# Moving a normalization from VectorE to ScalarE in the preparation of a four-layer graph network

## The reference

```
h = maximum(layernorm(x), 0)                    # (6250, 128)
edge_feat = concat(h[src], h[dst])              # (106250, 256)
g = gelu(edge_feat @ mlp_w1 + mlp_b1)           # 64 hidden
w = sigmoid(g @ mlp_w2 + mlp_b2)                # one weight per edge
...                                             # degrees from w, then
out = segment_sum((h @ conv_w)[src] * norm, dst) + conv_b
x = x + out                                     # three more layers of this kind
```

## Time and profile before

| | |
|---|---|
| median of 3 runs | 4262.63 us (4259.69 to 4265.24) |
| the profiled execution, own time | 4269.07 us |
| its span, first to last instruction | 4267.3 us |
| mean granted clock of TensorE | 0.804 |
| busy share: PE, DVE, ACT, POOL | 75%, 52%, 46%, 52% |
| preparation, to the end of line 1442 | 119.3 us |

### The profile page before, as it was taken

One profiled execution on the slowest core, in us unless ns is written; L12 is line 12 of the kernel. 1 busy time (PEld: TensorE's weight loads), 2 busy tenths in 40 slices (PEclk: granted clock), 3 DMA queues, 4 the chain that ended last, 5 costly groups with the idle time before them and its releaser, 6 DMA issues.

```text
span 4267.3 us, 68479 instructions
## 1 busy us (share of the span) xinstructions
PE 3218.4 (75%) x19874; PEld 2621.2 (61%) x19874; DVE 2219.3 (52%) x9829; ACT 1973.3 (46%) x2929; POOL 2238.3 (52%) x1830
## 2 busy tenths in 40 slices
PE   4666667644454466676899419998999999999999
PEld 3455555433333355565687317887777788888888
DVE  6766666544444599998211001266444444444444
ACT  2222222211111255555899419964444455555555
POOL 3777777777777888888888888811000000000000
PEclk6555555555555599998999759999999999999999
DMA  4899997444444599995999549964776788888897
GB/s 132 287 310 310 302 314 220 109 109 106 100 107 108 131 233 235 232 235 118 222 240 264 112 64 255 260 193 151 218 221 205 218 264 255 252 263 253 273 295 245
DMA packets 874024, 898.42 MB, mean 211 GB/s; under 512 B 186010, under 2 KB 807169, under 8 KB 873664
## 3 DMA queue, kind: packets, MB, share of 16 engines
q1 hardware_dynamic: 700656, 785.25, 59.4%
q0 software_dynamic: 168464, 107.01, 15.4%
q10 hardware_dynamic: 4544, 1.77, 0.2%
HBM read 699.91 MB, written 193.86 MB: 209 GB/s over the span
## 4 chain that ended last, share of the span: by engine, by line
PE 40%; POOL 30%; issue 13%; DVE 12%; DMA 4%; ACT 1%; SPq 0%; DVEq 0%; POOLq 0%; ACTq 0%
PE ps L1191 27%; POOL adj L792 22%; POOL rows L784 8%; PE ps L1096 5%; PE ps L1078 3%; DMA adj<-scattering 3%; DVE same L1456 2%; DVE pre L1492 1%; DMA pieces<-adj 1%; DVE scaled L1496 1%; DVE wide L1808 1%; PE ps L1259 1%; PE ps L1264 1%; ACT wide L977 1%; PE ps L1187 1%
## 5 line engine op out<-in xcount | busy, mean ns | idle before, releaser
L1191 PE MATMUL ps<-wide,tab 128*128 128x512 f32 (+2 forms) x7644 | 1730.1, 383 | 50.7 <-DVE wide L1808 42.1
L1191 PEld LDWEIGHTS ps<-wide,tab 128*128 128x128 f32 x7644 | 1373.7, 189 | 355.4 <-DVE wide L1808 63.0
L977 ACT CAST wide<-pieces 128x1536 fp32r<-128x1536 f16 (+5 forms) x1026 | 1245.8, 1258 | 743.6 <-PE ps L1191 553.5
L792 POOL DMA_INDIRECT adj<-scattering x832 | 1310.1, 1575 | 253.7 <-issue 243.7
L784 POOL DMA_INDIRECT rows<-table,src_of x880 | 843.6, 959 | 319.3 <-issue 260.0
L1808 DVE CAST wide<-pieces 128x1024 fp32r<-128x1024 f16 (+3 forms) x604 | 397.0, 663 | 577.0 <-PE ps L1191 573.8
L1096 PE MATMUL ps<-dst_mlp,onehot_t 128*128 x2640 | 364.5, 232 | 142.1 <-DVE pre L1492 92.5
L824 POOL DMA_DIRECT2D out<-scattering x13 | 9.8, 754 | 838.3 <-DVE scattering L1773 838.3
L1096 PEld LDWEIGHTS ps<-dst_mlp,onehot_t 128*128 128x128 bf16 x2640 | 274.9, 104 | 221.8 <-issue 163.5
L1456 DVE SCALAR_TENSOR_TENSOR same<-ps,key,first_weight 128x128 bf16<-128x128 f32 x832 | 284.9, 344 | 228.3 <-PE ps L1078 227.9
L908 ACT ACTIVATE onehot<-plain,norm 128x128 f32<-128x128 bf16 x880 | 280.9, 390 | 227.0 <-DVE norm L1562 227.0
(11 more groups left out here) (262 smaller groups left out, 3542.1 us busy)
## 6 DMA issues: line engine op xcount, KB each, us to landing
pieces<-adj SPq DMA_DIRECT2D x550, 640.0 KB, 5.3
pieces<-adj SPq DMA_DIRECT2D x121, 512.0 KB, 4.8
h_rows<-rows SPq DMA_DIRECT2D x220, 256.0 KB
rows<-h_rows SPq DMA_DIRECT2D x220, 256.0 KB
onehot_list<-onehot_b SPq DMA_DIRECT2D x220, 128.0 KB, 2.8
low_row<-low_list SPq DMA_DIRECT2D x220, 128.0 KB
plain<-onehot_list SPq DMA_DIRECT2D x220, 128.0 KB
pieces<-adj SPq DMA_DIRECT2D x54, 480.0 KB, 4.6
```

The source lines that it names most:

```text
L792: nc.gpsimd.indirect_dma_start(out=adj[:, :], out_offset=bass.IndirectOffsetOnAxis(ap=place[:, k:k + 1], axis=0), in_=count16[:, k:k + 1], ...
L977: nc.scalar.copy(to, of).then_inc(cast_act, 1)
L1191: last = nc.tensor.matmul(ps_sum[SUMMED[u] % 2][:, 0:b * P], tab[q % 2][:, c, half, :], of, start=(c == u0 and half == 0), stop=(kind == " ...
```

## The change

- ScalarE writes h itself, one instruction per block, from x: Relu(x * rstd - mean * rstd), scale and bias per partition. For the bias, invert_roots computes node_shift = -mean * rstd on VectorE. norm_nodes leaves VectorE and relu_nodes ScalarE; the semaphore node_fed goes, node_scaled comes.
- TensorE transposes h, so that the copy out of PSUM needs no Relu; this copy and all that follows it lags one chunk more.
- The first half's roots are inverted as soon as they are there; ScalarE takes the second half's roots in front of its fourth chunk (ROOTS_AT = 3).
- SyncE stores the edge lists between the two halves of x instead of behind x.
- The edge rows are read at chunk 6 instead of 8.
- The 23 later weights are issued behind the chunks on ScalarE's queue; TensorE waits for them in front of the first layer's end, ScalarE behind its last weighing.

```diff
+        node_shift = room[:, 0:NW]
...
-        STEPS_READ = 8
+        STEPS_READ = 6
+        ROOTS_AT = 3
...
             for k, (b0, b1) in enumerate(X_PIECES):
+                if k == len(X_PIECES) // 2:
+                    sp.wait_ge(rows_in, 16 * 6)
+                    for e in range(2):
+                        sp.dma_start(edge_list[e].rearrange("(c p) j -> p c j", p=P), rows_i[:, e, :, :]).then_inc(lists_stored, 16)
                 sp.dma_start(x[:, b0:b1, :], a["x"][b0 * P:b1 * P, :].rearrange("(b p) d -> p b d", p=P)).then_inc(x_in[k // 2], 16)
             sp.wait_ge(pads_set, 3)
             sp.dma_start(x[0:N % P, whole, :], a["x"][whole * P:N, :]).then_inc(x_in[-1], 16)
-            sp.wait_ge(rows_in, 16 * 6)
-            for e in range(2):
-                sp.dma_start(edge_list[e].rearrange("(c p) j -> p c j", p=P), rows_i[:, e, :, :]).then_inc(lists_stored, 16)
...
-            for where, what in loads:
-                act.dma_start(where, what).then_inc(weights_in, 16)
-            for n, (b0, b1) in enumerate(STAT):
+            def take_node_roots(n):
+                b0, b1 = STAT[n]
                 act.wait_ge(variances, n + 1)
                 nc.scalar.activation(node_rstd[:, b0:b1], node_rstd[:, b0:b1], ACT.Sqrt).then_inc(roots_set, 1)
-            def relu_nodes(i):
+            def take_later_roots(i):
+                if i == ROOTS_AT:
+                    take_node_roots(1)
+            def norm_nodes(i):
                 b0, b1 = node_blocks(i)
-                act.wait_ge(node_fed, i + 1)
-                nc.scalar.activation(h[:, b0:b1, :], node_pre[:, i % 2, 0:b1 - b0, :], ACT.Relu).then_inc(h_set, 1)
+                act.wait_ge(node_scaled, 1 if b1 <= STAT[0][1] else 2)
+                for b in range(b0, b1):
+                    last = nc.scalar.activation(h[:, b, :], x[:, b, :], ACT.Relu, bias=node_shift[:, b:b + 1], scale=node_rstd[:, b:b + 1])
+                last.then_inc(h_set, 1)
...
-                nc.scalar.activation(node_t[:, i % 2, 0:(b1 - b0) * P], ps_node_t[:, i % 2, 0:(b1 - b0) * P], ACT.Relu).then_inc(node_turned_sb, 1)
+                nc.scalar.copy(node_t[:, i % 2, 0:(b1 - b0) * P], ps_node_t[:, i % 2, 0:(b1 - b0) * P]).then_inc(node_turned_sb, 1)
...
-            pipeline(MC, [(2, take_first_part), (0, relu_nodes), (0, copy_nodes)])
+            take_node_roots(0)
+            pipeline(MC, [(0, take_later_roots), (3, take_first_part), (0, norm_nodes), (1, copy_nodes)])
+            for where, what in loads:
+                act.dma_start(where, what).then_inc(weights_in, 16)
...
-            act.wait_ge(weights_in, 16 * LOADS)
             act.wait_ge(steps_set, 1)
...
             for g in range(GROUPS):
                 weigh(g)
+            act.wait_ge(weights_in, 16 * LOADS)
...
             def turn_nodes(i):
                 b0, b1 = node_blocks(i)
-                pe.wait_ge(node_fed, i + 1)
+                pe.wait_ge(h_set, i + 1)
                 after(pe, node_turned_sb, i - 1)
                 for b in range(b1 - b0):
-                    last = nc.tensor.transpose(ps_node_t[:, i % 2, b * P:(b + 1) * P], node_pre[:, i % 2, b, :], ident[:, :])
+                    last = nc.tensor.transpose(ps_node_t[:, i % 2, b * P:(b + 1) * P], h[:, b0 + b, :], ident[:, :])
...
-            pipeline(MC, [(0, turn_nodes), (1, multiply_nodes), (1, turn_steps)])
+            pipeline(MC, [(0, turn_nodes), (1, multiply_nodes), (2, turn_steps)])
...
-            pe.wait_ge(weights_in, 16 * LOADS)
             pe.wait_ge(zero_set, 2)
             add_no_degrees(True)
...
             pe.wait_ge(added, GROUPS * S)
+            pe.wait_ge(weights_in, 16 * LOADS)
...
                 link(nc.vector.reciprocal(node_rstd[:, b0:b1], node_rstd[:, b0:b1]))
+                nc.vector.scalar_tensor_tensor(node_shift[:, b0:b1], node_moments[:, b0:b1, 0], -1.0, node_rstd[:, b0:b1], ALU.mult, ALU.mult
+                                               ).then_inc(node_scaled, 1)
...
             nc.vector.tensor_copy(tile_of[:, :], ps_tile_t).then_inc(tile_of_set, 1)
+            invert_roots(0)
             dve.wait_ge(x_in[1], 48)
             node_stats_of(1)
-            invert_roots(0)
...
-            def norm_nodes(i):
-                b0, b1 = node_blocks(i)
-                after(dve, node_turned, i - 1)
-                after(dve, h_set, i - 1)
-                for b in range(b0, b1):
-                    last = nc.vector.tensor_scalar(node_pre[:, i % 2, b - b0, :], x[:, b, :], node_moments[:, b, 0:1], node_rstd[:, b:b + 1],
-                                                   ALU.subtract, ALU.mult)
-                last.then_inc(node_fed, 1)
...
-            pipeline(MC, [(2, take_src), (0, norm_nodes), (0, read_steps), (2, split_nodes), (3, take_steps)])
+            pipeline(MC, [(0, take_src), (0, read_steps), (0, split_nodes), (3, take_steps)])
```

More of the change, by code:

```diff
@@ L451, in build @@
         roots_set = sem("roots_set")
-        node_fed = sem("node_fed")
+        node_scaled = sem("node_scaled")
         h_set = sem("h_set")
```

## The result

The changed kernel took 4240.2 us (median of 5 runs, 4237.23 to 4243.74), the kernel before 4260.3 us (5 runs, 4259.38 to 4265.24): ratio 0.9949, 95% interval 0.9935 to 0.9964, that is 20.1 us faster, between 15.3 and 27.7. The forecast was 4238 (4230 to 4250). The profiled execution of the changed kernel took 4243.74 us, that of before 4269.07; these two lie 25.3 us apart.

The account below looks back on a forecast made before the run. The preparation ahead of the edge loop, paced by VectorE/TensorE to 762 us, was taken to set the end. Chunks from 32.0 plus 33.5 end at 65.5 instead of 90.34: 4262.63 - 24.8 = 4237.8 us, forecast 4238 (4230 to 4250).

Parts of the forecast that it names:

- The bound and its release: Preparation ahead of the edge loop: shorter by d, it ends the kernel d earlier if both starts move along.
- Loads: Start of the kernel: first half's statistics begin at 14.5 us (13.3 to 15.8) instead of 18.52, VectorE's first chunk at 32.0.
- the earlier landing of the lists: Loads at the start: without the weights between, the lists could land at 6.5 us instead of 9.05.
- The round: Walk through 13 chunks: a round is the largest engine's share, ScalarE's 2.35 us, not the sum of 4.4.
- the three cold rounds: Start of the chunk walk: TensorE at 1.2 GHz for about three rounds, adding 3 x 0.5 = 1.5 us.
- the slower rival: Chunk walk: stages stay in series, 6.3 us a round, 19 us late, 4282 us; decides from 4.5 us; chance 0.03.
- signs named for being wrong: Rounds over 3 us, ScalarE idle before first parts, another group loop or scatter pace, first edge copy waiting for ScalarE's queue.
- The clock: TensorE in the chunk walk: fewer pauses, so 1.2 GHz for about three rounds more, then rounds of 2.35 us.
- Due dates: Edge rows read at chunk 6 and weights issued behind the chunks cost nothing: 7 and at least 11 us of cover.
- the first term of the sum: End of the old chunk walk, line 1395, at 90.34 us; less the predicted 65.5 it gives 24.8 us.
- GpSimd's lead of 15.8 us: Edge loop to 762 us: GpSimd's 25 waits for line 1492, 15.8 us together, taken as up to that much lead.

Follow-up runs that it names:

- loop_alone: The changed kernel with its loads in their old places and edge rows read at chunk 8: 4242.62 us against 4261.7 for the kernel before, ratio 0.9953.
- move_no_lag: The changed kernel, normalization still on ScalarE, with the old lags: 4262.36 us, ratio 1.0001 to the kernel before.
- lags_alone: The kernel before with the new lags alone, VectorE still normalizing, now ahead of the taking: 4257.89 us, ratio 0.999.
- before_a: The kernel before, unchanged, profiled once more: walk 59.1 us, line 1395 at 86.2 us.
- experiment 3: Two runs of the changed kernel with GpSimd's first table gather made to wait longer: 4245.65 and 4259.47 us beside 4238.55.
- before_b: The kernel before, unchanged, profiled another time: walk 58.8 us, line 1395 at 86.8 us.
- again: The changed kernel, unchanged, run once more: 4238.55 us against 4259.57 for the kernel before, ratio 0.9951.
- gathers_late: The changed kernel with GpSimd's first table gather waiting for changed_set, beginning 14.3 us later: 4245.65 us beside 4238.55.
- gathers_later: The changed kernel with GpSimd's first table gather waiting for the keys, beginning 27.9 us later: 4259.47 us beside 4238.55.
- split_lag: The changed kernel with VectorE's splitting one chunk behind: 4239.74 us.
- lay_later: The changed kernel with splitting one chunk behind, ahead of the edge rows' reading, and the steps' layout behind two takings: 4239.31 us against 4259.39, ratio 0.995.

## Why the prediction was right, and where it was off

**The bound and its release.** That the preparation's end sets the end of all was right: the end of the walk, the keys and the first addition moved by 25.0, 25.0 and 25.1 us between the two profiles, the span by 25.3. The predicted 4244.2 for an execution like the profiled one met 4243.74. That the median of 4240.2 met 4238 as well has some luck in it: the gain was 20.1 us instead of 24.8, and the kernel before took 4260.3 us in five runs instead of the 4262.63 of three that the forecast started from.

**Loads.** The first statistics were predicted for 14.5 us, between 13.3 and 15.8, and came at 15.72: the upper bound. The term that failed is the earlier landing of the lists (8.94 us instead of 6.5 or a middle of it). With the weights out of the way they land as late as before, and from 6 to 8 us the DMA engines were busy only 0.39 of the time before and 0.38 after, which the mean of 0.86 over 18.5 us doesn't show. What the lists wait for stays open. x was early enough, as loop_alone shows from the other side (waits of 2.31 and 1.03 us come back). The first taking came at 32.98 instead of 32.0.

**The round.** Four normalizations took 1.65 us, as worked out; the round 2.27 instead of 2.35. Of the three cold rounds, a number that no row of before gives, one shows in VectorE's walk: it waits 1.00 us for TensorE at 38.33 us, where 1.5 were set aside. The walk from the first taking was 32.4 us instead of 33.5, while that taking came 1.0 late; so line 1395 met its 65.5 (65.34) by two small errors against each other. That the round would be the largest share and not the sum hangs on the lags. move_no_lag shows that the slower rival was a real mechanism: with the old lags a round took 4.09 us at the high clock and 5.36 at the low one, beyond the 4.5 from which it was to decide in part of the rounds only, and this ate the whole gain. There the trace agrees with the rule of the Trainium skill ("ScalarE: Activation LUTs", "Rules for kernel authors": relu, addition and multiplication belong on VectorE): four normalizations took 1.65 us on ScalarE against 1.11 on VectorE, and the move gained nothing. In the changed order the dearer engine was the right one, since 1.65 us ran beside the others' work and 1.11 us of VectorE would have been added to its 2.0 (lags_alone).

One of the signs named for being wrong did show: ScalarE is idle in front of six first parts, longest at 33.43 us (2.92) and 60.33 us (3.00). VectorE comes late there, behind the steps' layout, the last slow products of TensorE, the reading and the taking of the edge rows, or at the walk's end; the rounds between, such as the one from 41.08 us, have no such wait, so the stages don't stand in series.

**The clock.** The reason given for its level, the pauses, doesn't hold. before_a ran from 48.35 to 67 us at 1.00 with a pause of 1.61 us or more in every round (TensorE busy 9.30 of 18.65 us); the profile of before shows the same pauses at 0.50 from 43.75 to 73.5 us (busy 19.76 of 29.75). What decides between the two levels isn't shown by these runs. That the changed walk reaches the high one early was right in all of its profiles, but not for a reason that the rows of before could give.

**Due dates.** Edge rows read at chunk 6 were there (gathered by 40.3 us, read at 47.6); the weights' last issue ended at 76.3, long before 97.35; first edge work at 97.35 against 97.5 predicted.

**The step that was mis-sized** is the first term of the sum, 90.34 us. It was read from one profiled execution as if the kernel always walked that long. Four executions have line 1395 at 88.7 us in the mean, the keys at 116.0; against two executions of the changed kernel (65.4 and 93.7 in the mean) the gain is 23.2 and 22.3 us, not 24.8, and these executions lie 4266.9 - 4243.5 = 23.4 us apart. The timings say 20.1 and 21.0, with intervals that reach from 15 to 28. All four profiled executions of before (4263.27 to 4269.07 us) lie above its medians of 4259 to 4262, which isn't explained. Why lags_alone gained less in time (3.8 us) than by its keys (107.5 against 116.0) isn't settled either; its interval reaches to 8.1.

**The other one** is GpSimd's lead of 15.8 us, a sum of waits that the prediction took for time to spare. The group loop takes 1335 to 1340 us from the keys to the last addition in all runs but the two of experiment 3; in those it is 1357 us from the first gather, 19.5 us more. By that GpSimd was ahead by about 116.0 - 89.9 - 19.5 = 7 us before (first gather at 91.5, 87.4, 88.0 and 92.5) and 93.7 - 66.9 - 19.5 = 7 after. It didn't matter here, since the table's end moved as far as the keys.

## What to carry to other kernels

When engines stand idle in turn, look at the written order before the engines: a stage moved to another engine gained nothing until the lists let it run a chunk ahead, and then even a dearer engine paid. Count what each engine does in a round; the largest share is what is left once the series is broken, and a fixed block on another engine (the edge rows here) then decides how near one comes. A stage whose clock rises at another place in each execution has no single length: take several profiles of the kernel before, or a bound on either side, ahead of sizing the gain, and compare versions by rounds at the same clock. A sum of waits is not a lead; delay the one that is ahead and see.

## What the runs showed of the hardware

In the same walk of the same program TensorE worked at 1.2 GHz for 4 us in one execution (39.21 to 43.4 us, before_b) and for 35 us in another (38.36 to 73.5 us, before): the transposes first ran at 2.4 GHz at chunk 2, 3, 7 or 9. A round took 4.4 to 4.6 us at the low level and 3.17 at the high one. In the changed walk the level varied over the first five chunks; the transposes of the sixth took 0.66 us in every profile of it (after, again, loop_alone, gathers_late, gathers_later, split_lag, lay_later). In split_lag the granted clock was 1.00 from 47 to 49 us, into a pause of 1.85 us, and 0.50 from 50 to 53 us, while the products behind the pause ran (2.04 us instead of 1.14).

A ScalarE instruction with scale and bias both read per partition took 0.39 us in sequence on a 128x128 block (1.65 us for four), 0.07 more than the 0.32 of the form with one such operand.
